# Query/key staging and attention joined in one block, the rotated biases summed through PSUM, and y turned ahead of the mask matmuls in the expert stage

## The chip, the cores and the metric

One of the cores of one Trainium2 chip runs the kernel. The metric is the time of one execution in microseconds (us), as the device reports it. The engines are named as in the profile: PE is TensorE with PEld its weight loads, DVE is VectorE, ACT is ScalarE, POOL is GpSimd, and SP is SyncE, which here only starts DMA transfers. The engines run side by side; each works through its own queue in order, and they wait for one another on semaphores.

## What is computed

The reference is one layer of a vision model on `x` of shape (4, 64, 64, 64): batch, height, width, channels. Three parts follow one another, the second and the third each added to what came before:

```python
# windows of 8x8 tokens, 8 heads of 8 channels
qkv = xw @ qkv_w.T + qkv_b
q, k = _rope2(q), _rope2(k)                      # rotation by row and column position
attn = softmax(q * hd ** -0.5 @ k.T)
h = (attn @ v) @ proj_w.T + proj_b
# selective scan over 4096 positions on layernorm(h)
h = h + scan(layernorm(h), W_dbc, W_dt, b_dt, A_log, D)
# experts: each token picks one of 32
idx = argmax(xf @ router_w.T + router_b)         # xf = layernorm(h)
h1 = relu(xf @ W1[idx] + b1[idx])
h = h + relu(h1 @ W2[idx] + b2[idx])
```

## The kernel before

All data is float32 and stays on the core; `h_all` holds the 128 tiles of 128 tokens by 64 channels, handled as 32 quads of four tiles. There is no scheduler: each engine's program is written out by hand, and a `then_inc` on one engine is what a `wait_ge` on another waits for. Two instructions of one engine that depend on each other also have a semaphore between them. PSUM is one tile of eight banks.

**Block 1, weights, turns and q/k.** The weights and `x` are loaded. PE turns `x` in sixteen pieces of eight tiles (`turn_x(n)`, n from 0 to 15, four transposes each); ACT copies the even ones out of PSUM and DVE the odd ones, each twice (`copy_x`, lines 171 and 175), once by rows and once by columns. The rotation by position is built into the weights by POOL (lines 275 to 282) and into the biases by DVE: for q and for k, eight rotated biases are `cos * b + sin * b_swapped` (lines 396 to 402). Only eight pieces are turned before the q/k products begin; the others are turned between them. The products are 32 groups `m` (lines 360 and 362), each into one bank, which ACT and DVE empty half and half (`copy_qk`, lines 240 and 431), adding the bias. Product 0 needs the DVE copies of pieces 1, 3, 5 and 7. Once 16 products are copied, SP fetches the q and k of two quads into the attention's layout, and POOL makes the first masks (`mask_qk`, lines 484 and 486). Behind product 31 come small things for the scan: a product of weights on PE, its copy to `w_delta` on DVE, and `-exp(a_log)` on ACT and DVE (`a_neg`).

**Block 2, attention and scan.** A block ends when all engines have ended it. In attention, step `i` of each engine holds pieces of work for neighbouring quads: PE does the scores of quad i+1 (line 597), turns probabilities (612), multiplies them with v (628), makes the next v (661) and projects (669). DVE takes the maximum and subtracts it (762, 767) and normalises (775, 780); ACT does the exponentials and copies; POOL does a part of the layer norm (559 to 575) and the masks for quad i+2. A function `ahead(i)` puts other work between steps. On POOL it does, at i = 18, seventeen small operations that make constants for the scan, and at i = 20 seven that split `b2` in three bf16 parts. The scan follows, and is the same before and after.

**Block 3, experts.** One step `i` handles several quads at different depths. Quad i+1: ACT stages the scan's output `y_st`, PE turns it (line 1760), DVE adds it to `h_all` (1851), and DVE and POOL do the layer norm, which ends in `xh`. Quad i-1: PE turns `xh` (1744), ACT copies it to `x_t`, PE computes the router's logits (1765), and DVE finds the expert and marks it (1865 to 1882). Quad i-2: PE computes all experts' hidden values (1704), turns the marks (1727), ACT and DVE copy half of them each to `mark_t` (1800, 1832), and PE adds a large negative number by them where an expert isn't chosen (`mask`, 1696); ACT and DVE apply relu (1790, 1846), and PE multiplies with the second weights (1770, 1778). Quad i-3: PE turns the result (1736), and DVE adds it to `h_all` (1838), from where SP stores it.

## Time and profile before

| | us |
|---|---|
| median of 3 runs (608.54 to 611.0) | 610.61 |
| the profiled execution | 610.79 |
| its span | 609.0 |
| PE busy in the span | 541.0 (89%) |
| DVE busy | 493.6 (81%) |
| ACT busy | 403.9 (66%) |
| POOL busy | 349.8 (57%) |

The profiled execution's own time is 1.8 us longer than its span, which is what lies around the first and the last recorded instruction. A busy share is an average over stages in which different engines set the pace, so it doesn't say what a change is worth; the rows of single stages do. Block 1 takes the first 56 us, attention lasts to about 300, the scan to 396, and the experts to the end.

### The profile page before, as it was taken

What the parts mean: (1) busy time and instruction counts of PE and PEld (TensorE: products, weight loads), DVE (VectorE), ACT (ScalarE), POOL (GpSimd) and SP (SyncE); (2) the same over time, 40 slices, a digit from 0 to 9 for tenths busy, and PEclk for the clock granted to TensorE, in tenths of its full rate; (3) what the DMA queues carried; (4) which work ended last, traced back from release to release, by engine and by line L of the source; (5) the groups of instructions that cost most, each with busy time, mean ns of one, the idle gap of its engine ahead of it and who ended that gap; (6) DMA issues with size and microseconds to landing.
All of it is one profiled execution on the core that took longest, in us unless ns stands there. A gap on an engine that the chain in (4) does not pass through costs nothing. (4 is left out here: it accounts for less than half of the span.)

```text
span 609.0 us, 18377 instructions
## 1 busy us (share of the span) xinstructions
PE 541.0 (89%) x7273; PEld 391.1 (64%) x7274; DVE 493.6 (81%) x911; ACT 403.9 (66%) x723; POOL 349.8 (57%) x388
## 2 busy tenths in 40 slices
PE   5797999999999999999557676759999999999996
PEld 4797889999988899998212232435555555555553
DVE  4887688888888888885798999858888888888873
ACT  3575788888888888889596676325454545454543
POOL 8303367777779877774799499653333333333320
PEclk9898799999999999999797889869999999999999
DMA  9732222222222222210000000000010101111111
GB/s 193 111 43 46 55 59 64 56 61 59 57 61 58 56 62 59 55 44 10 1 0 0 0 1 1 3 2 18 18 28 20 26 21 25 22 23 23 24 23 27
DMA packets 62382, 23.06 MB, mean 38 GB/s; under 512 B 45780, under 2 KB 62292, under 8 KB 62292
## 3 DMA queue, kind: packets, MB, share of 16 engines
q1 hardware_dynamic: 61200, 21.63, 17.5%
q8 instruction: 60, 0.98, 0.7%
q10 hardware_dynamic: 964, 0.20, 0.2%
q14 instruction: 30, 0.25, 0.1%
q0 software_dynamic: 128, 0.00, 0.0%
HBM read 5.02 MB, written 4.19 MB: 15 GB/s over the span
## 5 line engine op out<-in xcount | busy, mean ns | idle before, releaser
L762 DVE TENSOR_REDUCE work<-psum 128x16 f32<-128x1024 f32 x64 | 78.0, 1220 | 31.6 <-PE psum L597 31.6
L697 ACT ACTIVATE work<-work 128x1024 f32<-128x1024 f32 x64 | 67.8, 1060 | 23.1 <-DVE work L767 23.1
L767 DVE TENSOR_TENSOR work<-psum,work 128x1024 f32<-128x1024 f32 x64 | 78.4, 1225 | 2.2
L705 ACT ACTIVATE work<-psum 128x512 f32<-128x512 f32 x128 | 70.9, 619 | 3.1 <-PE psum L612 2.2
L612 PE MATMUL psum<-kc,work 128*128 128x128 f32 x512 | 68.6, 278 | 3.2 <-ACT work L697 2.8
L1681 POOL TENSOR_TENSOR m_rstd<-m_var,m_mhalf 128x4 f32<-128x4 f32 x32 | 32.2, 1008 | 61.9 <-DVE m_var L1889 61.9
L628 PEld LDWEIGHTS psum<-work 128*64 128x64 f32 x2048 | 62.3, 138 | 5.4 <-issue 5.1
L628 PE MATMUL psum<-work 128*64 128x18 f32 x2048 | 65.5, 212 | 0.0
L612 PEld LDWEIGHTS psum<-kc,work 128*128 128x128 f32 x512 | 59.8, 143 | 7.5 <-ACT work L697 2.9
L1704 PE MATMUL psum<-x_t,w1x 64*64 64x256 f32 x1024 | 64.4, 390 | 0.0
L484 POOL TENSOR_TENSOR work<-work,kc 128x512 f32<-128x512 f32 x32 | 41.9, 1309 | 38.5 <-DMA work<-big_bc 26.8
L1790 ACT ACTIVATE hid<-psum,b1c 128x512 f32<-128x512 f32 x96 | 58.9, 685 | 7.5 <-PE psum L1696 7.5
L1778 PE MATMUL psum<-hid,w2x 128*64 128x256 f32 x512 | 60.7, 379 | 0.4 <-ACT hid L1790 0.4
L559 POOL TENSOR_TENSOR work<-work 128x4 f32<-128x4 f32 x32 | 32.6, 1018 | 41.6 <-DVE work L793 41.4
L1704 PEld LDWEIGHTS psum<-x_t,w1x 64*64 64x64 f32 x1024 | 32.7, 134 | 28.7 <-issue 12.6
L1800 ACT ACTIVATE mark_t<-psum 96x256 bf16<-96x256 f32 x32 | 12.1, 379 | 58.1 <-PE psum L1727 58.1
L1679 POOL TENSOR_TENSOR m_sq<-m_xc 128x256 f32<-128x256 f32 x32 | 19.6, 612 | 53.9 <-DVE m_xc L1860 53.8
L1778 PEld LDWEIGHTS psum<-hid,w2x 128*64 128x64 f32 x512 | 34.7, 136 | 15.2 <-ACT hid L1790 0.6
L486 POOL TENSOR_TENSOR work<-work,kc 128x512 f32<-128x512 f32 x32 | 41.2, 1286 | 0.0
L597 PE MATMUL psum<-work 32*128 32x128 f32 x1024 | 38.8, 289 | 2.3 <-PEq L187 1.5
L597 PEld LDWEIGHTS psum<-work 32*128 32x128 f32 x1024 | 32.6, 191 | 7.9 <-issue 7.9
L669 PE MATMUL psum<-w_out,work 128*128 128x256 f32 x128 | 36.2, 405 | 0.5 <-ACT work L723 0.5
(198 smaller groups left out, 1281.2 us busy)
## 6 DMA issues: line engine op xcount, KB each, us to landing
work<-big_bc SPq DMA_DIRECT2D x256, 32.0 KB, 2.0
h_all<-in_x SPq DMA_DIRECT2D x16, 256.0 KB, 5.3
work<-big_a SPq DMA_DIRECT2D x32, 128.0 KB, 2.2
out<-out_st SPq DMA_DIRECT2D x126, 32.0 KB
w1x<-in_L_ffn_W SPq DMA_DIRECT2D x2, 128.0 KB, 4.2
kc<-constants SPq DMA_DIRECT2D x1, 202.0 KB, 2.8
w2x<-in_L_ffn_W SPq DMA_DIRECT2D x1, 128.0 KB, 3.5
work<-in_L_tok_qkv_w ACTq DMA_DIRECT2D x2, 32.0 KB, 3.5
```

The source lines that it names most:

```text
L484: pool.tensor_tensor(t["k_st"][:, :, :, :, :].rearrange("p f b h k -> p (f b) h k"), k, head, ALU.mult).then_inc(t["k_masked"], 1)
L486: pool.tensor_tensor(t["q_st"][:, :, :, :].rearrange("p f b (w k) -> p (f b) w k", w=2), q, win, ALU.mult).then_inc(t["q_masked"], 1)
L597: m = pe.matmul(banks[g][:, at:at + P], q_st[q, f, b, :], k_st[q, f, b, :, :], start=True, stop=True, skip_group_check=True)
L612: m = pe.transpose(banks[4 + half][:, n * P:n * P + P], prob[:, f, at:at + 2, :], ident)
L628: m = pe.matmul(banks[6][64 * w:64 * w + 64, at:at + 18], prob_t[:, f, n * 2 + b, 64 * w:64 * w + 64], v_st[:, par, 2 * f + b, w, n, :], s ...
L697: act.activation(prob[:, f], prob[:, f], ACT.Exp).then_inc(prob_done, 1)
L705: act.activation(prob_t[:, f, 4 * half:4 * half + 4, :].rearrange("p j q -> p (j q)"), banks[4 + half][:, :], ACT.Copy).then_inc(prob_t_do ...
L762: dve.tensor_reduce(top[:, f, :].rearrange("p (g h) -> p g h", g=4), sc, AX.X, ALU.max).then_inc(top_done, 1)
L767: dve.tensor_tensor(prob[:, f].rearrange("p (g h) k -> p g h k", g=4), sc, top[:, f, :].rearrange("p (g h) -> p g h", g=4).unsqueeze(3).br ...
L1704: m = pe.matmul(psum[64 * c:64 * c + 64, HID_BANK[g], 256 * b:256 * b + 256], w1x[q, g * 8 + 4 * c:g * 8 + 4 * c + 4, :], x_t[q, i % 2, :, ...
L1778: m = pe.matmul(psum[64 * b:64 * b + 64, 6, 0:256], w2x[:, g, :], hid[:, g, 256 * b:256 * b + 256], start=False, stop=(g == 3), skip_group ...
L1790: act.activation(hid[:, g, :], psum[:, HID_BANK[g], :], ACT.Relu, bias=b1c[:, g:g + 1]).then_inc(relu_act, 1)
```

## The change

Four things are edited.

The rotated biases: the cosine products of q and k are written to PSUM, in columns of bank 1 that nothing else uses at that time, and one operation each multiplies by the sine and adds the PSUM operand. The scale of q's swapped bias is put in when it is copied. The instructions that DVE runs between its copies of pieces 3 and 5 are, before:

```order
L171 COPY big_a<-psum 128x32x4x4
L175 COPY u_all<-psum 128x4x32x4
L396 TENSOR_SCALAR work<-kc,work 128x8
L398 TENSOR_SCALAR work<-kc,work 128x8
L402 TENSOR_TENSOR work<-work 128x8
L396 TENSOR_SCALAR work<-kc,work 128x8
L398 TENSOR_SCALAR work<-kc,work 128x8
L402 TENSOR_TENSOR work<-work 128x8
L171 COPY big_a<-psum 128x32x4x4
L175 COPY u_all<-psum 128x4x32x4
```

and with the change:

```order
L170 COPY big_a<-psum 128x32x4x4
L174 COPY u_all<-psum 128x4x32x4
L405 TENSOR_SCALAR psum<-kc,work 128x8 x2
L410 SCALAR_TENSOR_TENSOR work<-kc,work,psum 128x8 x2
L170 COPY big_a<-psum 128x32x4x4
L174 COPY u_all<-psum 128x4x32x4
```

Lines 171 and 175 (170 and 174 with the change) are the two copies of a piece; the six operations between them are now four, and each of the four has an operand in `psum`.

One block: q/k staging and attention are now in one block, without the meeting of all engines between them. Each engine waits instead for what it needs of the others: SP, and PE ahead of its first v product, wait for all 32 q/k copies; PE waits for `wd_copied`; ACT and POOL wait for `mean_done`, `scan_in` and `a_done`. The small things for the scan move in between the products: `exp` behind m = 20 on ACT, the weight product behind m = 23 on PE, `w_delta` and the negation behind m = 24 on DVE.

POOL's constants: what was at i = 18 and i = 20 now stands behind the first masks, ahead of attention. POOL's program at that place, before:

```order
L484 TENSOR_TENSOR work<-work,kc 128x512
L486 TENSOR_TENSOR work<-work,kc 128x512
L187 UNCONDITIONAL_BRANCH
L1212 UNCONDITIONAL_BRANCH
L553 MEMSET work 128x4
L484 TENSOR_TENSOR work<-work,kc 128x512
L486 TENSOR_TENSOR work<-work,kc 128x512
```

and with the change, from the first masks to the end of the constants' first part (then as many rows again, to the masks of the next quad):

```order
L491 TENSOR_TENSOR work<-work,kc 128x512
L493 TENSOR_TENSOR work<-work,kc 128x512
L1220 UNCONDITIONAL_BRANCH
L1222 MEMSET ones 128x1
L1223 MEMSET eps 128x1
L1225 MEMSET same 128x128
L1225 MEMSET w_b 128x128 x2
L1225 MEMSET w_c 128x128 x2
L1229 MEMSET same 64x64
L1231 COPY w_b<-wd 64x64
```

Lines 484 and 486 (491 and 493) are the masks. The 24 small operations of steps 18 and 20 have come between those of the first quad and those of the second.

The expert step: y is turned into the upper half of bank 2, where it was the lower half of bank 0, and ahead of the masks. (In these rows the experts' own semaphores carry an m_ in front.) Bank 2's lower half takes the marks that ACT copies, so the turn of y waits for that copy; and the turn of the marks, which writes bank 2, now waits until DVE has read the y before it. PE's step with all quads alive, with its waits, before:

```order
L1727 MATMUL psum<-ident_b,mark 96x128 [waits mark_dve,m_o_copied,mark_act,chosen]
L1727 MATMUL psum<-ident_b,mark 96x128 x3
L1736 MATMUL psum<-kc,m_o_t 128x128 [waits m_h_done]
L1736 MATMUL psum<-kc,m_o_t 128x128
L1744 MATMUL psum<-kc,m_xh 128x128 [waits lg_done,m_xh_done]
L1744 MATMUL psum<-kc,m_xh 128x128
L1696 MATMUL psum<-mark_t,off 128x512 [waits mark_dve,mark_act]
L1696 MATMUL psum<-mark_t,off 128x512 x3
L1760 MATMUL psum<-kc,y_st 128x128 [waits out_made,m_h_done,y_staged]
L1760 MATMUL psum<-kc,y_st 128x128
L1765 MATMUL psum<-rwx,x_t 128x64 [waits m_x_copied]
L1765 MATMUL psum<-rwx,x_t 128x64
```

and with the change:

```order
L1734 MATMUL psum<-ident_b,mark 96x128 [waits mark_dve,mark_act,m_o_copied,m_h_done,chosen]
L1734 MATMUL psum<-ident_b,mark 96x128 x3
L1744 MATMUL psum<-kc,m_o_t 128x128 [waits out_made]
L1744 MATMUL psum<-kc,m_o_t 128x128
L1752 MATMUL psum<-kc,m_xh 128x128 [waits lg_done,m_xh_done]
L1752 MATMUL psum<-kc,m_xh 128x128
L1761 MATMUL psum<-kc,y_st 128x128 [waits mark_act,m_h_done,y_staged]
L1761 MATMUL psum<-kc,y_st 128x128
L1702 MATMUL psum<-mark_t,off 128x512 [waits mark_dve,mark_act]
L1702 MATMUL psum<-mark_t,off 128x512 x3
L1773 MATMUL psum<-rwx,x_t 128x64 [waits m_x_copied]
L1773 MATMUL psum<-rwx,x_t 128x64
```

The pair for `y_st` (line 1760, now 1761) has gone from behind the masks (1696, now 1702) to the place between the pair for `m_xh` and the masks, and its wait for `out_made` is now one for `mark_act`.

The diff, cut to its core (indentation that changes because of the one block is left out):

```diff
@@ q/k block, SP, ACT and POOL
                     fetch_x(sp, at, 0)
+                    sp.wait_ge(qk_act, 32)
+                    sp.wait_ge(qk_dve, 32)
...
-                    act.wait_ge(scan_in, 16 * 9)
-                    act.activation(a_neg[:, :], a_neg[:, :], ACT.Exp).then_inc(a_done, 1)
+                        if m == 20:
+                            act.wait_ge(scan_in, 16 * 9)
+                            act.activation(a_neg[:, :], a_neg[:, :], ACT.Exp).then_inc(a_done, 1)
 
                     act.wait_ge(row_in, 48)
+                    act.wait_ge(mean_done, 2)
+                    act.wait_ge(a_done, 2)
...
                     mask_qk(pool, at, 0)
+                    pool.wait_ge(mean_done, 2)
+                    pool.wait_ge(scan_in, 16 * 9)
+                    pool.wait_ge(a_done, 2)
@@ PE
-                    pe.wait_ge(wdt_copied, 1)
-                    pe.matmul(banks[1][:, 0:C], wd_t[:, :], wdt[:, :], start=True, stop=True
-                              ).then_inc(wd_done, 1)
+                        if m == 23:
+                            pe.wait_ge(wdt_copied, 1)
+                            pe.matmul(banks[1][:, 0:C], wd_t[:, :], wdt[:, :], start=True, stop=True
+                                      ).then_inc(wd_done, 1)
+                    pe.wait_ge(wd_copied, 2)
@@ DVE
-                    dve.tensor_copy(bqk_swap[:, :], banks[1][:, 0:2]).then_inc(prep, 1)
+                    dve.tensor_scalar(bqk_swap[:, 0:1], banks[1][:, 0:1], SCALE, None, ALU.mult)
+                    dve.tensor_copy(bqk_swap[:, 1:2], banks[1][:, 1:2]).then_inc(prep, 1)
...
                     for qk in range(2):
-                        dve.tensor_scalar(rb_t[:, :], kc[:, K_COSC:K_COSC + 8], bqk[:, qk:qk + 1],
-                                          SCALE if qk == 0 else 1.0, ALU.mult, ALU.mult).then_inc(prep, 1)
-                        dve.tensor_scalar(rbias[:, qk, :], kc[:, K_SINC:K_SINC + 8], bqk_swap[:, qk:qk + 1],
+                        rb_cos = psum[:, 1, 16 * qk + 16:16 * qk + 24]
+                        dve.tensor_scalar(rb_cos, kc[:, K_COSC:K_COSC + 8], bqk[:, qk:qk + 1],
                                           SCALE if qk == 0 else 1.0, ALU.mult, ALU.mult).then_inc(prep, 1)
-                        done += 2
-                        dve.wait_ge(prep, done)
-                        dve.tensor_tensor(rbias[:, qk, :], rbias[:, qk, :], rb_t[:, :], ALU.add).then_inc(prep, 1)
-                        done += 1
-                        dve.wait_ge(prep, done)
+                    for qk in range(2):
+                        rb_cos = psum[:, 1, 16 * qk + 16:16 * qk + 24]
+                        dve.wait_ge(prep, 4 + qk)
+                        dve.scalar_tensor_tensor(rbias[:, qk, :], kc[:, K_SINC:K_SINC + 8], bqk_swap[:, qk:qk + 1], rb_cos,
+                                                 ALU.mult, ALU.add).then_inc(prep, 1)
+                    dve.wait_ge(prep, 7)
                     dve.sem_inc(bias_ready, 1)
...
+                        if m == 24:
+                            dve.wait_ge(wd_done, 1)
+                            dve.wait_ge(wd_zeroed, 1)
+                            for b in range(2):
+                                q = slice(64 * b, 64 * b + 64)
+                                dve.tensor_copy(w_delta[q, q], banks[1][q, 0:C]).then_inc(wd_copied, 1)
+                            dve.wait_ge(a_done, 1)
+                            dve.tensor_scalar(a_neg[:, :], a_neg[:, :], -1.0, None, ALU.mult).then_inc(a_done, 1)
+                    dve.wait_ge(scan_in, 16 * 9)
...
-            both_stages(nc, stages, t, work, (router_w, router_b, w1, b1, w2, b2))
+                both_stages(nc, block, stages, t, work)
@@ attention, PE
         def values(i):
             pe.wait_ge(x_staged, i * 16 + 16)
-            if not first(i):
+            if first(i):
+                pe.wait_ge(t["qk_act"], 32)
+                pe.wait_ge(t["qk_dve"], 32)
+            else:
                 pe.wait_ge(prob_t_done, i * 4)
@@ attention, POOL
-            def ahead(i):
-
-                if i == 18:
-                    pool.memset(ones[:, :], 1.0).then_inc(const_set, 1)
+        pool.memset(ones[:, :], 1.0).then_inc(const_set, 1)
...
@@ experts, PE
                     pe.wait_ge(chosen, i - 1)
+                    pe.wait_ge(h_done, min(i + 1, QUADS))
...
-                    pe.wait_ge(h_done, min(i + 1, QUADS))
+                    if not first(i, 3):
+                        pe.wait_ge(out_made, i - 3)
...
+                if live(i, -1):
+                    pe.wait_ge(y_staged, i + 2)
+                    if not first(i, -1):
+                        pe.wait_ge(h_done, i + 1)
+                    if live(i, 2):
+                        pe.wait_ge(mark_act, i - 1)
+                    for n in range(2):
+                        m = pe.transpose(psum[:, 2, 256 + n * P:256 + n * P + P], y_st[:, n, :], ident)
+                    m.then_inc(y_turned, 1)
                 if live(i, 2):
...
                     for g in range(4):
                         mask(g)
-                if live(i, -1):
-                    pe.wait_ge(y_staged, i + 2)
-                    if not first(i, -1):
-                        pe.wait_ge(h_done, i + 1)
-                    if live(i, 3):
-                        pe.wait_ge(out_made, i - 2)
-                    for n in range(2):
-                        m = pe.transpose(psum[:, 0, n * P:n * P + P], y_st[:, n, :], ident)
-                    m.then_inc(y_turned, 1)
@@ experts, DVE
-                    dve.tensor_tensor(h, h, psum[:, 0, 0:256].rearrange("p (s d) -> p s d", s=4), ALU.add
+                    dve.tensor_tensor(h, h, psum[:, 2, 256:512].rearrange("p (s d) -> p s d", s=4), ALU.add
                                       ).then_inc(h_done, 1)
```

## Rows read from the trace of the kernel before

**Rows 1.** The page: its first line.

```profile
span 609.0 us, 18377 instructions
```

**Rows 2.** Busy time by stretch: stretch, length, each engine (instructions), granted clock, DMA.

```profile
93.30:184.05 90.75, 90.75 (x1770) 81.99 (x1769) 77.86 (x105) 79.36 (x158) 70.94 (x79) 1.00 0.27 60
410.07:588.52 178.45, 173.74 (x1972) 103.41 (x1973) 147.40 (x435) 94.94 (x203) 65.17 (x88) 1.00 0.10 22
588.52:600.53 12.01, 11.46 (x131) 6.67 (x131) 6.98 (x19) 5.85 (x12) 0.64 (x2) 1.00 0.10 23
```

**Rows 3.** Timeline of the front: start us, us, engine, line, operation, operands, [idle before].

```profile
12.86 0.78 DVE L396 TENSOR_SCALAR work<-kc,work 128x8 f32<-128x8 f32 x1
...
15.30 0.62 DVE L402 TENSOR_TENSOR work<-work 128x8 f32<-128x8 f32 x1
...
18.18 0.69 DVE L171 COPY big_a<-psum 128x512 f32<-128x512 f32 x1
18.79 0.68 DVE L175 COPY u_all<-psum 128x512 f32<-128x512 f32 x1
...
20.20 0.22 DVE L427 SCALAR_TENSOR_TENSOR bias_c<-work,psum 128x64 f32<-128x64 f32 x1
...
14.37 1.54 POOL L282 TENSOR_TENSOR work<-work 64x256 f32<-64x256 f32 x2
...
11.82 1.97 PE L316 MATMUL psum<-kc,h_all 128*128 128x128 f32 x8 [0.21 <-DMA h_all<-in_x]
14.23 1.91 PE L316 MATMUL psum<-kc,h_all 128*128 128x128 f32 x8 [0.44 <-DMA h_all<-in_x]
```

**Rows 4.** Timeline at the seam of blocks 1 and 2.

```profile
54.27 0.43 PE L369 MATMUL psum<-work 16*128 16x64 f32 x2
56.20 1.48 PE L597 MATMUL psum<-work 32*128 32x128 f32 x32 [1.50 <-PEq L187]
...
63.39 2.09 PE L597 MATMUL psum<-work 32*128 32x128 f32 x32
...
55.06 0.47 DVE L441 COPY w_delta<-psum 64x64 f32<-64x64 f32 x2
...
57.80 1.23 DVE L762 TENSOR_REDUCE work<-psum 128x16 f32<-128x1024 f32 x1 [1.52 <-PE psum L597]
...
48.90 1.28 POOL L486 TENSOR_TENSOR work<-work,kc 128x512 f32<-128x512 f32 x1
```

**Rows 5.** By stretch, both pieces of POOL constants; then timeline of DVE reciprocals.

```profile
188.86:191.64 2.78, 2.78 (x49) 2.49 (x48) 1.86 (x6) 2.66 (x6) 2.60 (x18) 1.00 0.28 70
203.58:205.83 2.25, 2.25 (x44) 1.96 (x42) 1.35 (x6) 2.19 (x4) 1.82 (x8) 1.00 0.35 87
...
195.82 0.35 DVE L775 RECIPROCAL work<-psum 128x32 f32<-128x32 f32 x1
...
224.72 0.35 DVE L775 RECIPROCAL work<-psum 128x32 f32<-128x32 f32 x1
```

**Rows 6.** Timeline of one expert step.

```profile
452.38 0.39 PE L1736 MATMUL psum<-kc,m_o_t 128*128 128x128 f32 x2
...
452.47 0.38 ACT L1800 ACTIVATE mark_t<-psum 96x256 bf16<-96x256 f32 x1 [1.71 <-PE psum L1727]
...
452.58 0.42 DVE L1832 CAST mark_t<-psum 96x256 bf16<-96x256 f32 x1 [0.48 <-PE psum L1727]
452.60 0.38 PE L1744 MATMUL psum<-kc,m_xh 128*128 128x128 f32 x2
...
453.15 0.59 PE L1696 MATMUL psum<-mark_t,off 32*128 32x512 bf16 x4 [0.16 <-DVE mark_t L1832]
...
453.67 0.44 PE L1760 MATMUL psum<-kc,y_st 128*128 128x128 f32 x2
```

**Rows 7.** Busy time by stretch, where the granted clock is 0.50.

```profile
19.35:22.78 3.43, 3.21 (x30) 3.24 (x32) 1.73 (x7) 0.68 (x1) 1.36 (x3) 0.50 1.33 214
56.92:67.16 10.24, 7.49 (x82) 6.21 (x75) 6.30 (x6) 4.59 (x7) 3.89 (x4) 0.50 0.28 59
```

More of the change, by code:

```diff
@@ L823, in carve, with both_stages @@
     return take
-def both_stages(nc, ctx, t, work, moe):
-    router_w, router_b, w1, b1, w2, b2 = moe
+def both_stages(nc, block, ctx, t, work):
     w1x, w2x, b1c, b2p, b2r, rwx, rb_row, rw = (
@@ new lines, in _, with start @@
+                kept_back()
+                skip(pool, mine, BLOCKS, BLOCKS)
+        def start(n):
+            for s in (c_done, rec_done, out_done, y_added):
+                pool.wait_ge(s, n * BLOCKS)
+            pool.wait_ge(tail_y, n * 2 + 1)
+            pool.tensor_copy(a_n[:, :], a_neg[:, bass.ds(n, 1)]).then_inc(rep_staged, 1)
+            pool.wait_ge(rep_staged, n * 5 + 1)
+            for w, at in ((w_b[0], RANK), (w_c[0], RANK + NS)):
+                for b in range(2):
+                    q = slice(64 * b, 64 * b + 64)
+                    pool.tensor_copy(w[q, q], wd[q, bass.ds(n + at, 1)].to_broadcast([64, 64])
+                                     ).then_inc(rep_staged, 1)
+            pool.wait_ge(rep_staged, n * 5 + 5)
@@ L1555, in near @@
-            def near(n):
-                body(n * BLOCKS + (BLOCKS - 1), (BLOCKS - 1) % RING, True)
-                carry(n, (BLOCKS - 1) % RING)
-            rest(dve, mine, some, start, full, near, lambda states: dve.sem_inc(tail_y, 2 * states))
-            dve.wait_ge(tail_acc, 1)
-            dve.wait_ge(tail_y, 2 * NS + 1)
-            dve.tensor_copy(y_tail, carried).then_inc(y_tail_set, 1)
-            dve.wait_ge(y_tail_set, 1)
-            dve.tensor_tensor(y_tail, y_tail, psum[:, 7, 0:P].rearrange("p (a t) -> p a t", a=2), ALU.add
-                              ).then_inc(y_tail_set, 1)
+                skip(dve, mine, 0, BLOCKS)
@@ new lines, in _, with start @@
+                dve.sem_inc(tail_y, 2)
+        with dve.If(alive_of[1][0] > 0):
+            whole(BLOCKS)
+            carry(1, (2 * BLOCKS - 1) % RING)
+        with dve.Else():
+            with dve.If(alive_of[1][1] > 0):
+                body(BLOCKS, BLOCKS % RING, True)
+                carry(1, BLOCKS % RING)
+                skip(dve, mine, BLOCKS + 1, BLOCKS - 1)
+            with dve.Else():
+                skip(dve, mine, BLOCKS, BLOCKS)
+                dve.sem_inc(tail_y, 2)
+        def start(n):
+            dve.wait_ge(rep_staged, n * 5 + 5)
@@ new lines, in full, with near @@
+        def full(n):
+            whole(n * BLOCKS)
+            carry(n, (BLOCKS - 1) % RING)
+        def near(n):
+            body(n * BLOCKS + (BLOCKS - 1), (BLOCKS - 1) % RING, True)
+            carry(n, (BLOCKS - 1) % RING)
+        rest(dve, mine, some, start, full, near, lambda states: dve.sem_inc(tail_y, 2 * states))
+        dve.wait_ge(tail_acc, 1)
+        dve.wait_ge(tail_y, 2 * NS + 1)
+        dve.tensor_copy(y_tail, carried).then_inc(y_tail_set, 1)
+        dve.wait_ge(y_tail_set, 1)
```

1015 lines of the change are left out of this document (488 added, 527 removed).

## The prediction

> **What bounds the kernel now.** First the page's head, for the span to work against: 609.0 us [rows 1], in an execution of 610.79 us; so 1.8 us lie around the span. That execution is 0.2 us above the median of the three runs shown (610.61), so a change of the span can be taken off either. Next the busy time by stretch, to see which stage has one engine full. From 93.30 to 184.05 us, thirteen passes of attention, TensorE (PE) is busy for 90.75 of 90.75 us [rows 2]: a pass takes 90.75 / 13 = 6.98 us and PE sets it. In the expert stage 29 steps lie between 410.07 and 588.52 us, 6.153 us each, with PE busy 173.74 of 178.45 and no other engine over 147.40 [rows 2]: PE too, with small gaps. The last row matters most. The next two steps, which have no y left to turn and no layer norm left to do, take 12.01 / 2 = 6.005 us [rows 2]. The three places where PE is not full for its own sake are the front, the seam between two blocks, and two passes of attention.
>
> The timeline shows them. At the front VectorE (DVE) is late. Six operations on 8 columns stand between its copies of piece 3 and of piece 5 of x: the first starts at 12.86 us and takes 0.78 us, the last ends at 15.30 + 0.62 = 15.92 us. Copy 7 starts at 18.18 and ends at 18.79 + 0.68 = 19.47, and PE's first q/k matmul, which waits for it, follows [rows 3]. PE had turned pieces 4 and 5 by 11.82 + 1.97 = 13.79 and pieces 6 and 7 by 14.23 + 1.91 = 16.14 [rows 3]. So DVE owns the front, by some 2 us. At the seam PE ends its last product at 54.27 and begins the first scores at 56.20, after DVE has copied w_delta (55.06) and every engine has met the block's end; DVE's first maximum starts at 57.80, 1.60 after the scores began. GpSimd (POOL) had finished the masks that scores need at 48.90 + 1.28 = 50.18 [rows 4]. Nothing but the block's end holds the scores back.
>
> **The change, part by part.** *Rotated biases.* Six operations become four; one tiny scaling is added where DVE then waits for PE anyway, so it costs nothing; without that cover it would cost about 0.15. The price of the four is not in the trace, since nothing there writes so few columns into PSUM from VectorE. From below: VectorE's operation that also reads PSUM, L427, takes 0.22 us [rows 3]; four, one behind the other, 0.88. From above: the mean of the six, (15.92 - 12.86) / 6 = 0.51, four 2.04. What decides between them is a coincidence in the rows: POOL's two adds start at 14.37 and take 1.54, so they end at 15.91, and the DVE add next to them, which has both inputs and its output in SBUF, ends at 15.92 [rows 3]. It stretches to POOL's end. All four new operations have one operand in PSUM and one tensor in SBUF, as L427 has; I take 0.88. Then they end at 13.74 and copy 5 starts when its pieces are turned, 13.85. From copy 7 counted backwards: it starts 18.18 - 15.92 = 2.26 after the biases' end, of which some 0.15 is the wait at their end, so copy 5 to copy 7 is 2.11, and 13.85 + 2.11 = 15.96. Copy 7 then waits for PE, 16.14 + 0.05 = 16.19, in place of 18.18: **2.0 us**. ScalarE's bias wait moves with it. The other end of the bounds: four at 0.51 end at 14.90, copy 7 starts at 17.16, which leaves 1.0.
>
> The Trainium skill (SBUF — State Buffer, "Who interferes with whom") says that a VectorE instruction with at most one SBUF input, outside the two-port modes, does not contend with GpSimd. By that rule the four are free of POOL, as in the choice made from the rows. Against the change speaks another page of the Trainium skill, VectorE: DVE Perf Modes ("The TRN2 errata"): a PSUM source costs 120 cycles where an SBUF source costs 58, at 0.96 GHz 65 ns more. By that table the four would be an estimated 0.26 us later than from SBUF, and the sum would not move, since copy 5 waits for PE until 13.85 whatever they take up to 0.99 us.
>
> *One block in place of two.* The weight product moves from behind the last q/k product to the middle, for PE two short matmuls (0.43 us from start to end [rows 4]); I add 0.2 us to the stream there. PE then goes straight on to the scores, from about 54.5 instead of 56.20. VectorE's two copies (0.47 us [rows 4]) and a negation of 16 columns go into its stream at m = 24. The negation may stand behind POOL's mask operation, which ends at 50.18; then VectorE is about 1.1 us late at m = 25 and gains back some 0.1 per product, PE's pace there being longer than its own operation. It would end product 31 near 55.7 and do its three constants until 55.95. If scores take what they took, 1.48 us, plus 0.12, the first maximum could start at 56.1; at a higher clock at 55.8. I take 55.9 against 57.80: **1.9 us**, with 1.6 to 2.1 as bounds. Behind it the chain is the old one: maximum, subtraction, exponential, PE's first turn. Queued behind the new waits are: on SyncE the fetch of quad 2, which waited for the seam anyway and now for the last q/k copies; on ScalarE nothing until the first exponential; on PE the values of quad 0, needing the same last copies, while the scores run ahead of them.
>
> *POOL's constants.* They leave passes 18 and 20. There they take 2.78 and 2.25 us of the clock [rows 5]. What they cost is read from VectorE's reciprocal: 195.82 to 224.72 is 28.90 us for four passes, where four of 6.98 are 27.92 [rows 5]: **1.0 us** given back. In their new place, 5.03 us from 50.2 on, they end at about 55.5 with a memset behind, and the second masks can't start before the first scores are over, some 55.7. Hidden, by little; and their reader, the second scores, started only at 63.39 [rows 4], 7.19 behind the first, of which the masks need 2.5, so 2 us more would also be hidden.
>
> *Expert step.* PE's pair that turns y leaves its place behind the masks (453.67, 0.44 us for the pair) for the place in front, where PE waits: its xh pair starts at 452.60, 0.22 behind the pair before it, and the masks start at 453.15, because DVE's mark_t ends at 452.58 + 0.42 = 453.00 [rows 6]. The new pair shares a bank with the marks that ScalarE copies, so it waits for that copy: 452.47 + 0.38 = 452.85, say 452.92 at PE. It holds PE for 0.22 (the pitch of two such pairs, 452.38 to 452.60) to 0.44 (the pair alone). So the masks begin at 453.15, their old time, to 453.36: a delay of 0 to 0.21. I take 0.02, since PE takes the next instruction at the pitch. Behind the masks a step then looks as the ones without y do: 6.005 us. That holds VectorE too: its wait before mark_t is 0.48 of each step [rows 6], so it can give 0.15. Gain per step 6.153 - 6.005 - 0.02 = 0.128, times 29: **3.7 us**; bounds 29 x (0.148 - 0.21) = -1.8 and 29 x 0.148 = 4.3. The extra wait for h on the turned marks is for work a whole step old; the relu operations are as before.
>
> **Sum.** 2.0 + 1.9 + 1.0 + 3.7 = 8.6; 610.8 - 8.6 = 602.2 us. One thing is in none of the terms: the granted clock. It is 0.50 (1.2 GHz) from 19.35 to 22.78, at the start of q/k, and from 56.92 to 67.16, around the first passes [rows 7]. Earlier starts meet these stretches elsewhere. In the second PE is busy 7.49 us [rows 7] and would need about half at 2.4 GHz, so at most 3.7 us could be gained; the first holds 3.21 us of work [rows 7], and one twice as long would lose 1.6. I put both at nothing in the sum and let them into the range.
>
> **The rivals.** (a) The expert pair isn't hidden: PE drains before the masks and 0.15 of each step stays. Then 3.7 goes and the time is 605.9. For it: the pair's own 0.44; against it: the pitch of 0.22. 0.13. (b) The clock is kept through the seam because PE has no 1.5 us pause there; half of the 3.7 gives 600.3. Against it: PE still pauses some 3 us for the first exponential. 0.12. (c) The biases stay tied to POOL, and POOL's constants delay the second masks: 602.2 + 1.0 + up to 1 = 604. 0.10. (d) The other side: the y pair waits in PE's queue not for ScalarE's first copy but in effect for its second, x_t, one operation later (about 0.55 on). Then masks, relus and outputs all shift by about 0.57 and the step is 6.57: 29 x 0.42 = 12.2 lost, 4.9 won, 618.1. It decides when the masks start over 0.32 us late, where 4.9 + 29 x 0.148 are used up. The new wait names the first copy's count, so only 0.02. (e) The change does in effect nothing at the seam and the front, since something else arrives just then (a load, an instruction fetch): 610.8 - 4.7 = 606.1. 0.05. The forecast itself has 0.58.
>
> **How the numbers follow.** Differences under 0.5% (3.05 us) can hardly be told from no change here. The forecast's own range, with the clock's smaller shifts, is 600 to 604.5; with (b) below and (a), (c) and (e) above it reaches from 599.6 to 606.2. Faster by over 0.5% means under 607.6: 0.93. Within 0.5%, two of the cases together: 0.05. Slower: 0.02.
>
> **What would show it.** In the changed profile: the first q/k matmul at about 17.6; four bias operations of at most 0.25 each; first scores about 2.0 + 1.7 earlier than 56.20, so at 52.5; VectorE's reciprocals 6.98 apart through all of attention; the y pair between xh and masks with about 0.02 to 0.1 of idle ahead, masks 1.03 to 1.05 behind the marks' turn, and an expert step of 6.02. The prediction is wrong if masks start more than 0.1 later than that, if copy 7 still ends long after pieces 6 and 7 are turned, or if a low clock lasts over more of q/k.

## The result, and the profile after

The changed kernel takes 605.67 us (median of 10 runs, 603.93 to 607.45) where the kernel before takes 609.92 (median of 10 runs on the same chip). The ratio is 0.9925, with a 95% interval of 0.991 to 0.9941: 3.6 to 5.5 us faster, 4.3 by the medians. Forecast were 8.6 us and 602.2, with a range of 599.6 to 606.2. The sign and the range held; half of the gain is missing, and that the range held was partly luck (see below).

The profiled execution took 605.85 us, its span is 604.1, against 609.0 [rows 1]. First the timeline of the front, as in [rows 3]:

```profile
12.86 0.35 DVE L405 TENSOR_SCALAR psum<-kc,work 128x8 f32<-128x8 f32 x2
...
13.12 0.36 DVE L410 SCALAR_TENSOR_TENSOR work<-kc,work,psum 128x8 f32<-128x8 f32 x2
...
13.86 0.69 DVE L170 COPY big_a<-psum 128x512 f32<-128x512 f32 x1 [0.39 <-PE psum L322]
...
14.30 1.10 PE L322 MATMUL psum<-kc,h_all 128*128 128x128 f32 x8 [0.48 <-DMA h_all<-in_x]
...
15.96 0.69 DVE L170 COPY big_a<-psum 128x512 f32<-128x512 f32 x1
...
17.35 0.45 PE L366 MATMUL psum<-big_a,work 128*64 128x128 f32 x1 [1.61 <-issue]
```

The four bias operations end at 13.48; copy 5 then waits 0.39 for PE, and copy 7 starts at 15.96. The first q/k matmul is at 17.35; in the kernel before it was at 19.57, so 2.22 us are won.

The seam, as in [rows 4]:

```profile
52.32 0.27 PE L368 MATMUL psum<-u_all,work 128*64 128x128 f32 x1
...
52.52 1.17 PE L604 MATMUL psum<-work 32*128 32x128 f32 x32
...
53.84 1.23 DVE L772 TENSOR_REDUCE work<-psum 128x16 f32<-128x1024 f32 x1 [0.28 <-PE psum L604]
...
53.98 1.26 POOL L491 TENSOR_TENSOR work<-work,kc 128x512 f32<-128x512 f32 x1 [0.40 <-PE psum L604]
...
59.42 2.09 PE L604 MATMUL psum<-work 32*128 32x128 f32 x32
```

The last q/k matmul of the kernel before was:

```profile
54.07 0.27 PE L362 MATMUL psum<-u_all,work 128*64 128x128 f32 x1
```

No wait for a block's end stands ahead of the scores: from the start of the last q/k matmul to the first scores it is 0.20 us, where it was 56.20 - 54.07 = 2.13. The first maximum starts 3.96 us earlier than before, of which 2.22 come from the front. POOL's constants are over before the second masks, which wait for PE's scores and for nothing else.

Attention by stretch (twelve passes, as in [rows 2]), and DVE's reciprocals where the constants used to be, as in [rows 5]:

```profile
93.93:177.69 83.76, 83.76 (x1634) 75.68 (x1633) 71.87 (x97) 73.13 (x144) 65.39 (x73) 1.00 0.27 59
...
191.65 0.35 DVE L785 RECIPROCAL work<-psum 128x32 f32<-128x32 f32 x1
...
219.57 0.35 DVE L785 RECIPROCAL work<-psum 128x32 f32<-128x32 f32 x1
```

83.76 / 12 is 6.98 again, and 191.65 to 219.57 is 27.92 us for four passes, where it was 28.90: the constants' 0.98 is back.

The expert stage by stretch, 29 steps with y and then two without, and below it the timeline of one step, as in [rows 6]:

```profile
403.96:583.61 179.65, 179.34 (x1971) 104.75 (x1971) 147.27 (x435) 94.92 (x202) 64.85 (x88) 1.00 0.10 22
583.61:595.62 12.01, 11.46 (x131) 6.66 (x131) 6.99 (x19) 5.85 (x12) 0.80 (x2) 1.00 0.10 23
```

```profile
452.34 0.42 PE L1734 MATMUL psum<-ident_b,mark 128*96 128x128 bf16 x4
...
452.60 0.39 PE L1744 MATMUL psum<-kc,m_o_t 128*128 128x128 f32 x2
452.69 0.38 ACT L1808 ACTIVATE mark_t<-psum 96x256 bf16<-96x256 f32 x1 [1.71 <-PE psum L1734]
...
452.81 0.42 DVE L1840 CAST mark_t<-psum 96x256 bf16<-96x256 f32 x1 [0.34 <-PE psum L1734]
452.83 0.38 PE L1752 MATMUL psum<-kc,m_xh 128*128 128x128 f32 x2
...
453.19 0.20 PEld L1761 LDWEIGHTS psum<-kc,y_st 128*128 128x128 f32 x2 [0.21 <-issue]
453.22 0.41 PE L1761 MATMUL psum<-kc,y_st 128*128 128x128 f32 x2
...
453.55 0.11 PEld L1702 LDWEIGHTS psum<-mark_t,off 32*128 32x128 bf16 x4 [0.17 <-issue]
453.56 0.60 PE L1702 MATMUL psum<-mark_t,off 32*128 32x512 bf16 x4
```

Here is the miss. A step takes 179.65 / 29 = 6.195 us, not 6.02: longer than the 6.153 of before. ACT's copy of the marks ends at 452.69 + 0.38 = 453.07; the y pair starts at 453.22, 0.88 behind the marks' turn (452.34); the masks start at 453.56, 1.22 behind it, where they were 1.03. The profile writes "issue" for both gaps in the weight loads, though the first is a wait for ACT: the program waits there for a semaphore that had been set just then. In the first step of the stage the profile does name it: the y pair there starts at 403.62, after 0.22 of idle put down to ACT's mark_t. The two steps without y still take 6.005.

Added up: front 2.22; seam to the fifth reciprocal (98.09 before, 93.93 after) 4.16 - 2.22 = 1.94; constants 0.99; from there to the first masks of the experts, mostly the scan, where no line was changed, 0.96; the 29 expert steps -1.20. Together 4.9, the difference of the spans.

### The profile page after: what moved, and what is told of

It is laid out like the page before. It is cut to its first block and busy times, and to the rows that moved or that the text cites. A ratio compares the mean times of both kernels' runs of the same rounds, so it can differ in the third digit from the quotient of the medians.

```text
span 604.1 us, 18372 instructions
## 1 busy us (share of the span) xinstructions
PE 542.7 (90%) x7273; PEld 389.6 (65%) x7274; DVE 491.1 (81%) x910; ACT 403.3 (67%) x723; POOL 350.0 (58%) x388
## 3 DMA queue, kind: packets, MB, share of 16 engines
q1 hardware_dynamic: 61200, 21.63, 17.6%
## 5 line engine op out<-in xcount | busy, mean ns | idle before, releaser
L1710 PEld LDWEIGHTS psum<-x_t,w1x 64*64 64x64 f32 x1024 | 32.8, 135 | 28.7 <-issue 12.6
L1854 DVE TENSOR_SCALAR hid<-psum,b1c 128x512 f32<-128x512 f32 x32 | 24.0, 751 | 15.6 <-PE psum L1702 15.6
```

The lines of the kernel that those rows point to most:

```text
L1710: m = pe.matmul(psum[64 * c:64 * c + 64, HID_BANK[g], 256 * b:256 * b + 256], w1x[q, g * 8 + 4 * c:g * 8 + 4 * c + 4, :], x_t[q, i % 2, :, ...
```

## The experiments

Each was set beside runs of the kernel before on the same chip. The kernel before had medians of 610.42 us beside y_first, y_first_twice, old_expert and expert_only, 609.12 beside consts_back, and 610.25 beside the others, so kernels are compared by their ratios, and medians of different chips only roughly. (A ratio here lies nearer to the quotient of the means than to that of the medians, so it can't be had from the medians shown.) "Step" and "masks" are read from the profiles; "masks" is the time from the start of the marks' turn to the start of the masks.

```
kernel            median   ratio to before (95%)      step    masks
changed           605.67   0.9925 (0.991  to 0.9941)  6.20    1.22
y_first           599.82   0.9844 (0.982  to 0.9868)  6.00    1.03
y_first_act_wait  604.98   0.9933 (0.9911 to 0.9955)  6.20    1.22
y_first_twice     606.34   0.9943 (0.9921 to 0.9965)  6.22    1.24
old_expert        603.51   0.9918 (0.9894 to 0.9941)  6.15    1.03
expert_only       610.39   1.0013 (1.0001 to 1.0026)  6.20    1.22
seam_only         607.83   0.998  (0.9963 to 0.9997)  6.15    1.03
old_bias          608.30   0.9979 (0.9965 to 0.9993)  6.20    1.22
sbuf_bias         607.16   0.9962 (0.9948 to 0.9976)  6.20    1.22
consts_back       606.11   0.9952 (0.9934 to 0.997)   6.20    1.22
```

### The expert edit alone, both ways

**old_expert** undoes the three parts of the expert edit in the changed kernel (place of the y pair, bank, waits); **expert_only** makes them in the kernel before. The former, cut to its core:

```diff
-                if live(i, -1):
...
-                    if live(i, 2):
-                        pe.wait_ge(mark_act, i - 1)
-                    for n in range(2):
-                        m = pe.transpose(psum[:, 2, 256 + n * P:256 + n * P + P], y_st[:, n, :], ident)
...
                     for g in range(4):
                         mask(g)
+                if live(i, -1):
...
+                    for n in range(2):
+                        m = pe.transpose(psum[:, 0, n * P:n * P + P], y_st[:, n, :], ident)
```

> The changed kernel with the expert edit alone undone (y pair behind the masks, bank 0). Theory A (the expert edit costs 0.042 us a step): expert step 6.15, 1.2 us faster than the changed kernel, 604.4 us, ratio to the kernel before 0.990 to 0.992. Rival (the expert step's 6.20 comes from elsewhere, such as the new order of code ahead of it): step 6.20 again and 605.6 us.

> The kernel before with the expert edit alone. Theory A: expert step 6.19 to 6.20 rather than 6.15, 1.2 us slower than the kernel before, 611.1 us, ratio 1.001 to 1.003; masks 1.2 us behind the marks' turn. As my prediction had it: step 6.02, 3.7 us faster, ratio 0.994.

The steps are as theory A has it: 6.15 without the edit and 6.20 with it, whatever stands ahead. expert_only is 0.1 to 1.6 us slower than the kernel before, where the 29 steps give 1.2. (The span of its single profile is 0.6 us shorter than that of the kernel before, by a scan that took 1.7 less; see the last section.) The times of old_expert alone show nothing: by the ratios it is 0.4 us faster than the changed kernel, with intervals that overlap, by the medians 2.2. The two profiles' spans are 3.0 apart (601.1 and 604.1), of which the 29 steps and the first masks are 1.4, and 1.5 is the clock at the start of q/k (last section).

### The same pair in another place

```diff
@@ PE, expert step, behind the turn of the marks
+                if live(i, -1):
+                    pe.wait_ge(y_staged, i + 2)
+                    if not first(i, -1):
+                        pe.wait_ge(h_done, i + 1)
+                    if i >= 4:
+                        pe.wait_ge(out_made, i - 3)
+                    for n in range(2):
+                        m = pe.transpose(psum[:, 0, n * P:n * P + P], y_st[:, n, :], ident)
+                    m.then_inc(y_turned, 1)
                 if live(i, 3):
...
@@ PE, expert step, behind the xh pair
-                if live(i, -1):
-                    pe.wait_ge(y_staged, i + 2)
-                    if not first(i, -1):
-                        pe.wait_ge(h_done, i + 1)
-                    if live(i, 2):
-                        pe.wait_ge(mark_act, i - 1)
-                    for n in range(2):
-                        m = pe.transpose(psum[:, 2, 256 + n * P:256 + n * P + P], y_st[:, n, :], ident)
-                    m.then_inc(y_turned, 1)
```

The wait for h on the turned marks goes back to the o pair too, and DVE reads y from bank 0. Every wait of the pair was there already or is for something older.

> The changed kernel with the expert step's y pair in a third place: right behind the turn of the marks, ahead of the pair for o, in bank 0 as in the kernel before, with waits that were all there already; the masks then stand right behind the turn of xh, as they did before. Theory A (the step lost because the y pair sits in the one gap of TensorE's queue that the masks' wait left too little room for, and pushes the masks 0.19 us back): masks 1.03 to 1.05 behind the marks' turn again, expert step 6.00 to 6.04 rather than 6.20, which over 29 steps is 4.6 to 5.8 us, so 600 to 601 us, ratio to the kernel before 0.983 to 0.985. Theory B (it isn't the place but the bank or the new waits for the marks' copies): the bank is the old one here and the wait for mark_act is gone, so the step is 6.00 to 6.04 too; B is told from A by the next kernel and by the masks' start. Theory C (nothing is won by any place, since the time from the masks to the last of the step takes the 0.13 back elsewhere): step 6.15 or more, 604 us or more. Risk: the pairs for o and xh come 0.20 to 0.25 later here, and if the wait for xh isn't long enough to take that in, masks go back by as much.

The timeline of a step of y_first:

```profile
456.46 0.42 PE L1733 MATMUL psum<-ident_b,mark 128*96 128x128 bf16 x4
...
456.72 0.39 PE L1744 MATMUL psum<-kc,y_st 128*128 128x128 f32 x2
456.81 0.38 ACT L1808 ACTIVATE mark_t<-psum 96x256 bf16<-96x256 f32 x1 [1.71 <-PE psum L1733]
...
456.92 0.42 DVE L1840 CAST mark_t<-psum 96x256 bf16<-96x256 f32 x1 [0.34 <-PE psum L1733]
456.94 0.38 PE L1753 MATMUL psum<-kc,m_o_t 128*128 128x128 f32 x2
...
457.16 0.38 PE L1761 MATMUL psum<-kc,m_xh 128*128 128x128 f32 x2
...
457.47 0.12 PEld L1702 LDWEIGHTS psum<-mark_t,off 32*128 32x128 bf16 x4 [0.17 <-issue]
457.49 0.59 PE L1702 MATMUL psum<-mark_t,off 32*128 32x512 bf16 x4
```

and its expert stage by stretch, 28 steps with y and then three without:

```profile
403.46:571.58 168.12, 168.12 (x1904) 101.67 (x1905) 144.74 (x420) 91.93 (x196) 62.78 (x85) 1.00 0.10 23
571.58:589.59 18.01, 17.31 (x197) 10.08 (x197) 12.19 (x34) 8.95 (x18) 3.02 (x5) 1.00 0.11 24
```

The masks are back at 1.03 and the step is 168.12 / 28 = 6.004 us, the same as without y (18.01 / 3 = 6.003): the pair is hidden wholly, and PE is busy in all of the stretch. The kernel takes 599.82 us, just under the 600 to 601 expected and 8.1 to 11.0 us less than the kernel before, and its interval lies clear of the changed kernel's. The risk named in the expectation sat exactly on the edge. The masks' two conditions fall together: DVE's copy ends at 456.92 + 0.42 = 457.34, and the xh pair started 0.33 ahead of the masks. The next kernel shows how sharp that edge is.

```diff
-                    for n in range(2):
+                    for n in (0, 1, 0, 1):
                         m = pe.transpose(psum[:, 0, n * P:n * P + P], y_st[:, n, :], ident)
```

> As y_first, with the y pair's two transposes done twice (four in all, the same results): one pair's length more in the place that is supposed to be free. If TensorE has slack there of 0.4 us or more, the masks stand where they stand in y_first and the step is the same within 0.02; if the slack is used up by the first pair, the masks move back by up to 0.2 us and the step by as much, some 3 to 6 us on the whole, 604 to 607 us.

```profile
452.74 0.42 PE L1733 MATMUL psum<-ident_b,mark 128*96 128x128 bf16 x4
453.00 0.61 PE L1744 MATMUL psum<-kc,y_st 128*128 128x128 f32 x4
453.45 0.38 PE L1753 MATMUL psum<-kc,m_o_t 128*128 128x128 f32 x2
453.67 0.38 PE L1761 MATMUL psum<-kc,m_xh 128*128 128x128 f32 x2
453.98 0.60 PE L1702 MATMUL psum<-mark_t,off 32*128 32x512 bf16 x4
```

Two transposes more shift the masks by 0.21 and the step by 0.22. The slack in front of the masks is one pair, no more. And PE goes from xh to the masks in 0.31 although all of their inputs are there (DVE's copy ends at 453.63, 0.35 ahead of them), so that pitch isn't a wait for an input.

### Place, bank or wait

y_first differs from the changed kernel in three things at once: the pair's place, its bank, and the missing wait for ACT. This kernel puts the wait back alone, ahead of the last pair:

```diff
                     if not first(i, 1):
                         pe.wait_ge(lg_done, i - 1)
+                    if live(i, 2):
+                        pe.wait_ge(mark_act, i - 1)
                     for n in range(2):
                         m = pe.transpose(psum[:, 1, n * P:n * P + P], xh[:, 2 * n:2 * n + 2, :], ident)
```

> y_first (masks 1.03 behind the marks' turn, step 6.00, 599.8 us) with one wait more: the xh pair, the last pair ahead of the masks, waits for ACT's copy of the marks, as the y pair does in the changed kernel; the order of the pairs and the banks are those of y_first. Theory A2 (the wait for ACT's copy is the whole loss: a pair that starts after it stands 0.34 ahead of the masks whatever it is): the xh pair starts 0.85 to 0.88 behind the marks' turn, the masks 1.20 to 1.24, the step is 6.18 to 6.23 and the time 605 to 606.5 us, as in the changed kernel. Rival (the y pair's place between xh and the masks, or its half of the marks' bank, is the loss, and the wait only stands by it): masks at 1.03 to 1.08, step 6.00 to 6.05, 600 to 601.5 us.

```profile
456.87 0.42 PE L1733 MATMUL psum<-ident_b,mark 128*96 128x128 bf16 x4
457.13 0.39 PE L1744 MATMUL psum<-kc,y_st 128*128 128x128 f32 x2
457.36 0.38 PE L1753 MATMUL psum<-kc,m_o_t 128*128 128x128 f32 x2
457.75 0.41 PE L1763 MATMUL psum<-kc,m_xh 128*128 128x128 f32 x2
458.09 0.60 PE L1702 MATMUL psum<-mark_t,off 32*128 32x512 bf16 x4
```

With the order and the banks of y_first, the wait alone brings the last pair to 0.88, the masks to 1.22 and the step to 6.20, to the hundredth what the changed kernel has. So the wait for ACT's copy in front of the last pair is enough to make the whole loss. In both kernels the pair that starts after that copy stands 0.34 ahead of the masks, though it turns y into bank 2 in one and xh into bank 1 in the other. The time, 604.98, is at the lower end of the expected 605 to 606.5. (The reverse, the changed kernel's place and bank without the wait, was not run.)

### The front

**old_bias** puts the six old bias operations back, with the waits between them:

```diff
-                    for qk in range(2):
-                        rb_cos = psum[:, 1, 16 * qk + 16:16 * qk + 24]
-                        dve.tensor_scalar(rb_cos, kc[:, K_COSC:K_COSC + 8], bqk[:, qk:qk + 1],
...
+                        dve.tensor_scalar(rb_t[:, :], kc[:, K_COSC:K_COSC + 8], bqk[:, qk:qk + 1],
+                                          SCALE if qk == 0 else 1.0, ALU.mult, ALU.mult).then_inc(prep, 1)
+                        dve.tensor_scalar(rbias[:, qk, :], kc[:, K_SINC:K_SINC + 8], bqk_swap[:, qk:qk + 1],
...
+                        dve.tensor_tensor(rbias[:, qk, :], rbias[:, qk, :], rb_t[:, :], ALU.add).then_inc(prep, 1)
```

**sbuf_bias** keeps the four new ones and moves only the product for cos:

```diff
-                        rb_cos = psum[:, 1, 16 * qk + 16:16 * qk + 24]
+                        rb_cos = rb_t[:, qk, :]
```

> The changed kernel with the six old bias operations. If the count and the size of the bias operations are what the front waits for: first q/k matmul 2.0 to 2.2 us later (19.3 to 19.6 rather than 17.35), 607.7 us, ratio 0.995 to 0.9965. Rival (the first q/k matmul came earlier through TensorE's clock in its transposes of the pieces, 1.10 rather than 1.91, not through the biases): first q/k matmul by 0.8 us later or less, 606 to 606.5 us.

> The changed kernel with the product for cos kept in SBUF rather than in PSUM; the four bias operations and their order stay. If PSUM is what makes them short (0.17 each, none of them beside a long operation of POOL's that it waits for): two or more of the four take 0.5 to 1 us as the old ones did, and the first q/k matmul comes up to 1 us later, 606.5 us. If it is only that there are four of them, one group behind the other, and not six with a wait behind each: 0.17 to 0.25 each and 605.7 us.

In old_bias the first q/k matmul is at 19.47, 2.12 later, although PE's transposes of pieces 6 and 7 took 1.09 there: the faster transposes alone give 0.1 at most (19.57 to 19.47), the biases the rest. The times of both kernels came out longer than expected (608.30 for 607.7, 607.16 for 606.5); the last section has a likely reason. In sbuf_bias it is at 18.63, so of the 2.12 us the destination in PSUM is worth 1.28 and the smaller number of operations 0.84. The timeline of sbuf_bias shows how:

```profile
12.76 0.73 POOL L279 TENSOR_TENSOR work<-work,kc 128x256 f32<-128x256 f32 x1 [0.18 <-POOL work L286]
12.83 1.36 DVE L406 TENSOR_SCALAR work<-kc,work 128x8 f32<-128x8 f32 x2
13.44 0.72 POOL L280 TENSOR_TENSOR work<-work,kc 128x256 f32<-128x256 f32 x1
14.11 0.88 DVE L411 SCALAR_TENSOR_TENSOR work<-kc,work 128x8 f32<-128x8 f32 x2
```

DVE's two operations of L406 on 8 columns take 0.69 and 0.77 one by one; the first ends at 13.52, with POOL's first operation (13.49), and the second at 14.19, with POOL's second (14.16). With the output in PSUM the same two take 0.22 each, 0.35 together since they overlap, beside the same operation of POOL's. The Trainium skill (SBUF — State Buffer, "Who interferes with whom") has this: a VectorE copy or tensor_scalar can enter a mode that takes the ports shared with GpSimd, and whoever issues second then blocks until the other instruction is over. The trace agrees with that rule: 0.69 and 0.77 against 0.22 us. The same section of the Trainium skill has a second sentence, for a VectorE instruction with two SBUF inputs beside a GpSimd instruction that reads SBUF, as L411 is here. Of its two operations only one shows it: the first, from 14.11, takes 0.22, the second, which starts at 14.24 with POOL's next operation, 0.74. The estimate from the Trainium skill's page VectorE: DVE Perf Modes ("The TRN2 errata") of 65 ns more for a PSUM source does not show here: L410 in the changed kernel, with one such source, takes 0.22 each time, and so does the short one of L411, with none.

### The seam and the constants

**seam_only** is the kernel before with the one block alone. **consts_back** is the changed kernel with POOL's constants back in steps 18 and 20:

```diff
-        pool.memset(ones[:, :], 1.0).then_inc(const_set, 1)
...
         def ahead(i):
-            pass
+            if i == 18:
+                pool.memset(ones[:, :], 1.0).then_inc(const_set, 1)
...
+            if i == 20:
+                pool.wait_ge(moe_in, 16 * 13)
```

seam_only is the changed kernel with old_expert's edit, old_bias's and this one together.

> The kernel before with the one block alone: old bias operations, old place of the y pair, POOL's constants back in the attention's last steps. My term for the seam was 1.9 us (bounds 1.6 to 2.1): 608.0 to 608.5 us, ratio 0.9965 to 0.9975, first scores 1.7 to 2.1 us earlier behind the last q/k matmuls than in the kernel before. Rival (most of the changed kernel's gain ahead of attention comes with the seam, the biases only moving a wait): 606 to 607 us.

> The changed kernel with POOL's constants back in steps 18 and 20 of attention, nothing else. My term: attention 1.0 us longer (the two quads that in the kernel before lay 7.4 to 7.6 rather than 6.98 apart come back), 606.7 us, ratio to the kernel before 0.994 to 0.995; the stretch at the seam as in the changed kernel. Rival (the constants at the seam delay the second quad's masks, so that taking them away wins there what is lost later): the second scores earlier than in the changed kernel and 605.7 us or less.

seam_only starts its q/k at 19.45 and its first maximum at 56.37 (57.80 before), so 1.31 us are won between them and 1.68 up to the fifth reciprocal (96.29 against 98.09). From its last q/k matmul to the first scores it takes 0.20 (54.85 to 55.05), as in the changed kernel, so 1.93 are won there, within the 1.7 to 2.1 expected. What the first maximum lacks is in the q/k products: from the first to the last they take 34.50 us in the kernel before and 35.40 here, but also 35.15 in expert_only, whose code is that of the kernel before up to there. Set beside expert_only, the first maximum gains 1.65. So the term is there, at its lower end; the ratio's interval, 0.2 to 2.3 us, holds it and excludes the rival's 3.3 and more. In consts_back the reciprocals around the constants stand at 190.30 and 219.17, 28.87 apart for four passes rather than 27.92: 0.95, the term as forecast. Its ratio is 1.6 us above the changed kernel's, with intervals that overlap, so it is the reciprocals that show the term. Its second scores start 6.89 us behind its first (51.19 and 58.08), and so they do in old_expert, which has the constants at the seam (50.90 and 57.79): the constants don't delay the second masks.

## Why the prediction was right, and where it was wrong

Three of the four terms came out as worked out; the fourth, the largest, has the wrong sign. Put right, the same sum lies above the forecast's range, so the range held partly by luck.

**Biases, 2.0: right, 2.22 measured.** Four operations, two that write PSUM and two that read it, were taken at 0.22, one behind the other. Each did take 0.22, but they overlap, and the four were over in 0.62; copy 5 then waited for PE as forecast (13.86 against 13.85). The prediction let copy 7 wait for PE until 16.19. Here PE's transposes took 1.10 instead of 1.91 us, so it started at 15.96, the time that the prediction had counted backwards. In consts_back, where they took 1.94, copy 7 does wait 0.33 for PE, until 16.13, and q/k starts at 17.52: the forecast's own 2.0. (Its estimate of 0.26 from the Trainium skill's table counts four PSUM sources where there are two; it changed nothing in the sum.) The upper bound of the cost, operations that stay tied to POOL, would have been real with the product in SBUF.

**One block, 1.9: right in the main.** Up to the fifth reciprocal 1.94 is measured in the changed kernel and 1.68 in seam_only. Up to the first maximum, for which the prediction gave 1.6 to 2.1, it is 3.96 - 2.22 = 1.74 and 1.31. The first scores are at 52.52 for a forecast of 52.5. **Constants, 1.0: right,** 0.98 in the reciprocals.

**Clock, at nothing: right at the seam.** The low clock there became shorter, 0.50 for 10.24 us before [rows 7] and 0.83 in the mean over the ten microseconds around the second scores of the changed kernel:

```profile
57.00:67.00 10.00, 8.97 (x145) 7.39 (x149) 6.93 (x8) 6.68 (x12) 2.55 (x2) 0.83 0.26 55
```

It gave 0.2 us: between the first maximum and the fifth reciprocal the gain grows from 3.96 to 4.16. Rival (b)'s 1.9 didn't come: the first reciprocal stands 12.6 us behind the first maximum in both kernels (57.80 to 70.42, 53.84 to 66.45). At the start of q/k the clock stayed low for some 3 us in both profiles, so it changed nothing between them, but it can (last section).

**Expert step, 3.7: wrong, -1.2 measured.** The step that failed is "The new pair shares a bank with the marks that ScalarE copies, so it waits for that copy [...] So the masks begin at 453.15, their old time, to 453.36: a delay of 0 to 0.21. I take 0.02, since PE takes the next instruction at the pitch." The delay was 0.19. That is inside the bounds given, as the -1.2 is (-1.8 to 4.3), and far from the value taken. Both of its parts were too small. The pair starts 0.88 behind the marks' turn, where the prediction's numbers give 452.92 - 452.12 = 0.80: ACT's copy ends at 0.73, and from there to PE it took 0.15, not 0.07. DVE's copy in [rows 6] had shown that very number: it ends at 453.00 and the masks start at 453.15. And the pitch from a pair of full transposes to the masks is 0.34, not the 0.22 from pair to pair; y_first_twice shows 0.31 with no wait at all. 0.88 + 0.34 = 1.22. The same sum with the right numbers would have been 6.195 - 6.153 = 0.04 lost a step, and the forecast 605.9 + 1.2 = 607.1, or 606.9 with the front's 2.2. That is over the range's upper end, 606.2, and 1.2 us over the measured 605.67. Of these 1.2 us 0.9 are the time that the prediction subtracts from: 610.8, one execution of the kernel before, where the median of ten runs is 609.92. In the pair of profiles it is instead the 0.96 ahead of the experts, which no edit explains. Rival (a), the pair not hidden, named the cause nearest to this one; it priced it at nothing lost, 605.9, and that this lies 0.2 from the measured time is luck too. Rival (d), a later operation of ACT's, did not happen. The other half of the term was right: behind the masks a step looks as one without y (the rest of it is 4.97 to 4.98 us in y_first and in the changed kernel, the step less the masks' time in the table). y_first earns it: 6.153 - 6.004 = 0.149 a step, the upper bound of the forecast.

## What to carry to other kernels

Work that is moved into a gap of another instruction's wait is free only if its own wait ends earlier than the one it hides behind by its whole length; read both ends against one start, and count the hop from the end of the producer to the engine from a row that shows it. Here the last pair had to start by 0.70, and the wait for ACT let it go at 0.88; the same pair two places earlier, with waits that were long satisfied, was worth 5 us more. And when short VectorE operations stretch to the end of a GpSimd operation beside them, look at where they write: moving the first two of the four outputs to PSUM took the four from 2.16 to 0.62 us here.

## What the runs showed of the hardware that was not expected

**The pitch depends on what follows.** From one pair of 128x128 transposes to the next PE takes 0.22 us, from a pair to the masks (32 rows, bf16 weights) 0.31 to 0.34, with a gap of 0.17 in the weight loads that has no releaser, in all eight kernels here whose masks don't wait for DVE (in the kernel before, seam_only and old_expert they do, and start 0.55 behind the pair). What makes the gap was not taken apart.

**The start of q/k has two levels.** The same 548 matmuls from the first q/k product to the first scores take 35.17 us in the changed kernel's profile and 33.67 in that of old_expert, whose code is the same up to there (rows of the changed kernel, then of old_expert):

```profile
17.35:20.35 3.00, 3.00 (x28) 3.00 (x30) 1.51 (x6) 0.68 (x1) 2.65 (x4) 0.50 1.33 219
...
17.35:52.52 35.17, 35.17 (x547) 33.11 (x547) 29.86 (x48) 25.70 (x40) 9.12 (x29) 0.96 0.42 68
```

```profile
17.23:50.90 33.67, 33.67 (x548) 31.61 (x548) 29.86 (x48) 25.68 (x40) 9.23 (x30) 1.00 0.44 72
```

In the first, PE begins q/k at the lower of the two levels, 1.2 GHz (0.42 us a matmul); in the second the granted clock is 1.00 throughout (0.27). How fast the transposes of pieces 6 and 7 ran doesn't decide it: they took 1.10 in the first, 1.64 in the second, and 1.09 in y_first_act_wait, which starts q/k at 2.4 GHz too. Nor does PE's pause ahead of q/k alone: 1.38 us in y_first, which starts at 1.2 GHz, and 1.45 in y_first_act_wait. Of the six profiles that start q/k by 17.6 us, four have the full clock; of the five that start it at 18.6 or later, after pauses of 1.89 us or more, none. So 1.5 us came with some of the early starts and not with others. That is likely why sbuf_bias and old_bias lie 2.3 and 3.3 us above the changed kernel by their ratios and only 1.3 and 2.1 by their first products, but the single runs have no trace that would show it.

**The scan wanders.** From the last reciprocal of attention to ACT's first copy of the marks it takes 122.81 us in the kernel before and 121.07 in expert_only, with the same code:

```profile
286.58 0.36 DVE L775 RECIPROCAL work<-psum 128x32 f32<-128x32 f32 x1 [4.68 <-PE psum L628]
...
409.39 0.38 ACT L1800 ACTIVATE mark_t<-psum 96x256 bf16<-96x256 f32 x1 [5.14 <-PE psum L1727]
```

```profile
286.36 0.36 DVE L775 RECIPROCAL work<-psum 128x32 f32<-128x32 f32 x1 [4.68 <-PE psum L628]
...
407.43 0.38 ACT L1802 ACTIVATE mark_t<-psum 96x256 bf16<-96x256 f32 x1 [5.09 <-PE psum L1728]
```

Over eleven profiles it lies between 121.07 and 123.50. On the page of the kernel before PE's granted clock moves between 0.6 and 0.9 from slice to slice in that stage; which of its drops falls on a matmul that is waited for was not looked into. The changed kernel has 121.66, 1.15 less than the kernel before and well within that spread (0.96 up to the first masks, which come 0.19 later there). So what its trace wins there can't be put down to the change.
